# Batch 0 of an attention and feed-forward layer: the second token half of Q and K placed by products with identity columns, W2's Hadamard transform one bank at a time

## Chip, cores and metric

The kernel runs on one core of a Trainium2 chip. The metric is the device time of one execution in microseconds (us). TensorE is called PE in the rows (its weight loads PEld), VectorE DVE, ScalarE ACT, GpSimd POOL; SP is the sync engine, which in this kernel issues every DMA.

## What is computed

The input is x of 4 batches by 512 tokens by 256 features, in float32. Each batch goes through one transformer layer:

```
x = x + layernorm(attention(layernorm(x)))      # 16 heads of 16, rotary positions, causal mask
x = x + layernorm(ffn(layernorm(x)))            # ffn: fwht(silu(x W1') * (x W3')) W2'
```

The attention softmax is over keys up to the query's own position. `fwht` is a Walsh-Hadamard transform of the 1024 hidden features, scaled by 1/32. The kernel folds it into W2 once, at the start, by transforming W2 in place of the hidden values.

## The kernel before

**Numbers in two parts.** Every operand of a product that needs float32 accuracy is held as a high part (the rounded fp32r word) and a low part (value minus high part). A product of two such operands is three products (`triple`, line 280).

**Q and K.** For each of four tiles of 128 tokens, `qkv` (line 399) makes the 512 columns of Q and K, ACT copies them (`copy_qk`), POOL and DVE apply the rotary positions (`rope_products`, line 851; `rope_cos` and `rotate`), PE transposes the result (`turn_qk`, line 426), ACT takes the high part (`qk_high`), DVE the low part (`qk_low`), into `qk_s`: 128 rows (8 heads of 16) by part, by chunk (2 of Q, 2 of K), by token. The scores use another layout. A head there has 48 rows, three for each of the 16 features: high, high, low for Q, and high, low, high for K, so that one product of 48 rows gives the three-term product. Two heads share 96 rows of `q_t`; in `k_t` each head has its own column block and the rows of the other head of the pair are zero. The kernel goes from the one layout to the other through HBM: `pack_qk` (line 298), run by SP, stores `qk_s` to `qk_scratch` in five DMAs per token half (`send`) and reads it back in three (`fetch_k` two, `fetch_q` one). For batch 0 the order is send(0), fetch_k(0), fetch_q(0), then a wait until all three fetches have landed (line 343), send(1), fetch_k(1), fetch_q(1), and after that `load_x(1)`. For batches 1 to 3 this runs beside the feed-forward part of the batch before. For batch 0 there is nothing before it.

**The score units.** The row maxima of the scores are needed before the exponentials. `UNITS` (line 63) is the list of this work: a "scores" unit is one bank of scores of query tile 0 (four heads), tile 1 (two heads), tiles 2 and 3 (one head); a "turn" unit transposes the maxima of a tile, which ACT then writes into rows 96 to 127 of `q_t`. Units 0 to 7 and 9 to 12 are the scores of tiles 0 and 1, which need the first token half alone; units 13 to 29 and 30 to 40 are those of tiles 2 and 3; units 8, 17, 34 and 41 are turns. PE makes a unit, DVE reduces it to maxima (line 1011), and the bank is then free again; batch 0 uses banks 4 to 7 in turn (`FIRST_UNIT_BANKS`). After unit 41, `attend(0)` (line 497) begins: scores transposed, exponentials, values.

**The order of work** is written out by hand: `FIRST_MIX` (line 106) for each engine's part of Q, K and V of batch 0 (q: product and copy, c and r: rotary on DVE, r on PE and ACT: transpose and high part, t: low part, b: values, e: POOL's part of the rotary), and numbers of units after which other work goes in. For batch 0: `FIRST_SELECTOR` (ACT's `select`, 1.9 us each), `BUTTERFLIES_BEFORE` (three stages of the transform of W2 on POOL, two instructions each, line 909), `FIRST_W2_PARTS`: "split" (ACT takes W2's high part, then POOL the low part in two halves, `w2_low`, line 922), "transform" (16 products with the 128 by 128 Hadamard matrix, line 630, into banks 0 to 3), "words" (ACT copies these four banks), "high" (ACT takes the high part of the result; DVE the low part in `iteration(0)`).

**The start.** POOL clears half of `k_t` (line 934), computes the roots of batch 0's first layernorm (`root`), then takes the low part of half of the Q, K and V weights (line 937), for which PE waits (`wqkv_l`). DVE normalizes (`norm_x`, line 1024), takes the low part of the other half of these weights (line 1152), the low parts of the transposed x (line 972) and of the biases (line 1115).

## Time and profile before

| | us |
|---|---|
| median of 3 runs | 493.75 |
| lowest and highest | 491.78, 494.93 |
| the profiled execution | 493.44 |
| its span | 491.7 |
| mean granted clock of TensorE | 0.89 of full speed |

The span is the time from the first to the last recorded instruction; the 1.7 us by which the execution is longer lie around it. Times in the rows count from the start of the span. A row of the timeline gives the start, the length, the engine, the line and the operation; "xN" merges N equal instructions, and the brackets say how long the engine had been idle and what ended that. A waiting instruction's recorded length can include its wait for a resource, which is how a blocked VectorE or GpSimd instruction shows. The clock of 0.50 is 1.2 GHz, 1.00 is 2.4 GHz.

### The profile page before, as it was taken

The page shows a single profiled execution, that of the slowest core. Times are in us where ns is not written, and L with a number is a line of the kernel's source. Part 1 is how long each engine was busy: PE and PEld are TensorE (multiplying, and loading weights), DVE is VectorE, ACT ScalarE, POOL GpSimd, SP SyncE. Part 2 cuts the span into 40 slices and gives each one's busy share as a digit, 9 for nine tenths or more (in the row PEclk, how much of TensorE's full clock was granted, in tenths as well). Part 3 has the DMA queues.
Part 4 walks back from the last instruction along what each step waited for, and adds up shares of the span by engine and source line. Part 5 has one row for each costly group of instructions (what it writes and reads, how often), then busy time and mean ns, then how long its engine had stood idle before and what let it go on. Part 6 is the DMA issues. An engine that isn't in the chain of part 4 may idle for free.

```text
span 491.7 us, 7737 instructions
## 1 busy us (share of the span) xinstructions
PE 406.4 (83%) x2786; PEld 334.9 (68%) x2786; DVE 282.7 (57%) x921; ACT 219.4 (45%) x332; POOL 179.3 (36%) x300
## 2 busy tenths in 40 slices
PE   5656396899599998997799989996899989838992
PEld 4445265459499985576699965585799965527992
DVE  7649377637646678267357677267367782451114
ACT  5436127744423248824423268533333378232221
POOL 5416532733512325614222246325032255132232
PEclk9985557999679999999599999998699999968996
DMA  7676700100785000202981002004950002000001
GB/s 227 221 194 192 171 0 1 45 1 1 204 220 133 1 2 20 67 2 92 231 199 36 2 0 87 1 1 155 239 122 2 1 0 87 0 2 0 1 1 43
DMA packets 35462, 36.94 MB, mean 75 GB/s; under 512 B 2016, under 2 KB 34528, under 8 KB 35424
## 3 DMA queue, kind: packets, MB, share of 16 engines
q1 hardware_dynamic: 35424, 36.45, 26.9%
q8 instruction: 22, 0.36, 0.3%
q14 instruction: 16, 0.13, 0.1%
HBM read 21.76 MB, written 14.68 MB: 74 GB/s over the span
## 4 chain that ended last, share of the span: by engine, by line
PE 58%; DVE 14%; ACT 8%; POOL 8%; issue 6%; DMA 4%; SPq 1%; POOLq 0%; DVEq 0%; ACTq 0%
PE ps L283 32%; PE ps L475 7%; PE ps L463 7%; PE ps L491 6%; DMA q_t<-qk_scratch 3%; ACT probs L704 2%; DVE masked_scores L1011 2%; POOL rstd_z L839 1%; PE ps L525 1%; DVE rot L998 1%; ACT L755 1%; ACT xy L752 1%; POOL w_s L927 1%; PE ps L432 1%; DVE qk_s L972 1%
## 5 line engine op out<-in xcount | busy, mean ns | idle before, releaser
L1011 DVE CUSTOM_DVE_ANT_0 masked_scores<-ps,mask_row 128x128 bf16<-128x128 f32 (+3 forms) x256 | 113.4, 487 | 53.3 <-PE ps L463 53.3
L283 PE MATMUL ps<-xt,w_s 128*128 128x256 f32 x768 | 113.6, 298 | 5.1 <-DVE xt L972 5.1
L283 PEld LDWEIGHTS ps<-xt,w_s 128*128 128x128 f32 x768 | 107.1, 205 | 7.2 <-DVE xt L972 6.9
L463 PE MATMUL ps<-k_t,q_t 96*128 96x128 f32 (+3 forms) x256 | 75.8, 385 | 18.6 <-DMA q_t<-qk_scratch 14.8
L866 POOL TENSOR_TENSOR hid_s<-gate,hid_s 128x512 fp32r<-128x512 f32 x32 | 41.2, 1288 | 120.5 <-ACT hid_s L716 120.5
L704 ACT ACTIVATE probs<-ps 128x1280 f32<-128x1280 f32 x64 | 76.6, 1237 | 11.3 <-PE ps L475 10.4
L463 PEld LDWEIGHTS ps<-k_t,q_t 96*128 96x128 f32 x256 | 47.0, 217 | 29.4 <-DVE maxima L1011 10.2
L475 PEld LDWEIGHTS ps<-q_t,k_t 128*128 128x128 f32 x256 | 44.6, 196 | 30.9 <-ACT probs L704 15.0
L475 PE MATMUL ps<-q_t,k_t 128*128 128x512 f32 (+3 forms) x256 | 54.7, 340 | 4.4 <-ACT probs L704 2.7
L283 PE MATMUL ps<-w_s,hid_s 128*128 128x256 f32 x384 | 54.1, 286 | 3.2 <-POOL hid_s L866 3.2
L283 PEld LDWEIGHTS ps<-w_s,hid_s 128*128 128x128 f32 x384 | 51.1, 193 | 4.3 <-POOL hid_s L866 3.6
L883 POOL TENSOR_SCALAR_AFFINE_SELECT probs<-probs 128x384 f32<-128x384 f32 x64 | 35.9, 561 | 30.8 <-ACT probs L704 30.8
L710 ACT ACTIVATE gate<-ps 128x512 f32<-128x512 f32 x32 | 19.1, 598 | 62.1 <-PE ps L283 62.0
L491 PE MATMUL ps<-probs,v_t 128*32 128x128 f32 (+3 forms) x512 | 43.6, 441 | 1.9 <-POOL probs L886 1.9
L283 PE MATMUL ps<-wqkv_s,q_t 128*128 128x512 f32 (+1 forms) x192 | 43.1, 365 | 1.8 <-ACT v_t L696 0.9
L1085 DVE TENSOR_TENSOR gate<-gate,ps 128x512 f32<-128x512 f32 x32 | 21.9, 685 | 35.7 <-ACT gate L710 35.6
L1018 DVE COPY o_t<-ps 128x512 f32<-128x512 f32 x16 | 11.1, 692 | 46.0 <-PE ps L491 45.6
L283 PEld LDWEIGHTS ps<-wqkv_s,q_t 128*128 128x128 f32 x192 | 32.5, 209 | 6.3 <-ACT v_t L696 1.5
L676 ACT ACTIVATE xt<-ps 128x256 fp32r<-128x256 f32 x32 | 12.1, 382 | 49.5 <-PE ps L534 34.6
L725 ACT ACTIVATE q_t<-ps 32x128 fp32r<-32x128 f32 (+3 forms) x40 | 17.9, 492 | 32.3 <-PE ps L457 32.2
L716 ACT ACTIVATE hid_s<-gate 128x512 fp32r<-128x512 f32 x32 | 20.2, 632 | 25.5 <-DVE gate L1085 22.3
L972 DVE TENSOR_TENSOR xt<-ps,xt 128x256 fp32r<-128x256 f32 x32 | 13.4, 420 | 26.9 <-ACT xt L676 26.6
(111 smaller groups left out, 504.5 us busy)
## 6 DMA issues: line engine op xcount, KB each, us to landing
qk_scratch<-qk_s SPq DMA_DIRECT2D x32, 256.0 KB, 3.5
k_t<-qk_scratch SPq DMA_DIRECT2D x16, 384.0 KB, 5.4
q_t<-qk_scratch SPq DMA_DIRECT2D x8, 768.0 KB, 8.7
qk_scratch<-qk_s SPq DMA_DIRECT2D x8, 512.0 KB, 3.2
xa<-in_x SPq DMA_DIRECT2D x4, 512.0 KB, 9.6
xy<-in_x SPq DMA_DIRECT2D x4, 512.0 KB, 3.6
out<-xy SPq DMA_DIRECT2D x8, 256.0 KB, 2.4
o_t<-in_w SPq DMA_DIRECT2D x1, 1024.0 KB, 10.3
```

Source lines behind the costliest of these rows:

```text
L283: ins = eng.matmul(o, lhs(i), rhs(j), start=first and n == 0, stop=last and n == 2, skip_group_check=skip)
L463: ins = pe.matmul(o[:, i * keys:(i + 1) * keys], q_t[0:QK_ROWS, h // 2, qt * P:qt * P + P], k_t[0:QK_ROWS, h, 0:keys], start=(i == 0), sto ...
L475: ins = pe.matmul(ps[:, col // 512, col % 512:col % 512 + n], k_t[:, h, kt * P:kt * P + P], q_t[:, h // 2, kt * P:TOKENS], start=(kt != 3) ...
L491: ins = pe.matmul(ps[32 * j:32 * j + 32, 6 + g % 2, kt * P:TOKENS], v_t[:, kt, h, :], probs[:, h % PROBS, KEY_COL[kt]:KEY_COL[kt] + TOKENS ...
L704: act.activation(probs[:, h % PROBS, :], src, ACT.Exp, scale=SCALE).then_inc(S["exp_done"], 1)
L710: act.activation(gate[:, a % 2, :], bank(2 * (a % 2)), ACT.Silu).then_inc(S["silu_done"], 1)
L716: act.activation(hid_s[:, a % 2, 0, :], gate[:, a % 2, :], ACT.Copy).then_inc(S["hid_h"], 1)
L866: pool.tensor_tensor(hid_s[:, a % 2, 1, :], gate[:, a % 2, :], hid_s[:, a % 2, 0, :].bitcast(F32), ALU.subtract).then_inc(S["hid_l"], 1)
L883: pool.affine_select(out=v, in_=v, compare_op=ALU.is_ge, fill=0.0, base=0, pattern=[[0, 3], [1, P]], channel_multiplier=-1)
L972: dve.tensor_tensor(dst, src, h.bitcast(F32), ALU.subtract).then_inc(S[done], 1)
L1011: ins = dve.tensor_tensor_reduce(masked_scores[:, SCORE_NO[n] % 2, i * keys:(i + 1) * keys], ps[:, banks[n], i * keys:(i + 1) * keys], mas ...
L1085: dve.tensor_tensor(gate[:, n % 2, :], gate[:, n % 2, :], bank(2 * (n % 2) + 1), ALU.mult)\
```

## The change

For batch 0 alone, the second token half of Q and K no longer goes through HBM.

- POOL clears a region of 2048 columns (the place of W3's low part, unused until later) and fills it by 12 small copies of identity columns: `choose_q` and `choose_k`, matrices that put each of a pair's 16+16 rows at its three places (between `root(0, "x")` and the weights' low part).
- `pick(n)`, 12 of them on PE: four products (two pairs or two heads, high and low part) of 96 columns of that matrix with 256 tokens of `qk_s`, into banks 0 to 3 in turn. `place(n)` copies such a bank into `q_t` or `k_t`: even n on ACT, odd n on DVE. `PICKS_BEFORE` says before which unit each stands, on all three engines.
- SP returns from `pack_qk(0)` after `fetch_q(0)`. So five stores, three fetches and the wait between the halves go, and `load_x(1)` is issued next.
- `FIRST_MIX` is in a new order, the selectors, butterflies and W2's split move, and the transform is done in four pieces of four products, after units 23, 26, 28 and 36, each with a copy of its own.

```diff
 FIRST_MIX = {
-    "PE": """q0 q1 r0 q2 q3 r1 b0 r2 b1 b2 b3 r3""".split(),
-    "ACT": """q0 q1 q2 r0 q3 r1 b0 b1 b2 r2 r3 b3""".split(),
-    "DVE": """c0 r0 c1 r1 t0 c2 c3 r2 t1 r3 t2 t3""".split(),
+    "PE": """q0 q1 r0 q2 q3 r1 b0 b1 r2 b2 b3 r3""".split(),
+    "ACT": """q0 q1 q2 r0 q3 r1 b0 b1 b2 b3 r2 r3""".split(),
+    "DVE": """c0 r0 c1 r1 t0 c2 r2 t1 t2 c3 r3 t3""".split(),
-FIRST_SELECTOR = {2: 0, 3: 2}
-BUTTERFLIES_BEFORE = [0, 4, 13]
-FIRST_W2_PARTS = {"split": 18, "transform": 33, "words": 36, "high": 38}
+FIRST_SELECTOR = {2: 21, 3: 38}
+PICKS = 12
+PICKS_BEFORE = [0, 0, 5, 9, 9, 10, 10, 10, 11, 11, 11, 11]
+BUTTERFLIES_BEFORE = [0, 2, 8]
+FIRST_W2_PARTS = {'split': 10, 'transform': [23, 26, 28, 36], 'words': [31, 33, 38, 38], 'high': 38}
...
                 sp.wait_ge(S["v_done"], b * TILES + TILES)
+                if b == 0:
+                    fetch_q(0)
+                    return
...
                 if kind == "scores" and qt == TILES // 2 and heads[0] == 0:
-                    pe.wait_ge(S["qk_in_late"], (b + 1) * 48)
+                    if b == 0:
+                        pe.wait_ge(S["placed_act"], PICKS // 2)
+                        pe.wait_ge(S["placed_dve"], PICKS // 2)
+                    else:
+                        pe.wait_ge(S["qk_in_late"], b * 48)
...
+            def pick(n):
+                if n == 0:
+                    pe.wait_ge(S["picks_made"], 1)
+                    pe.wait_ge(S["qk_l"], TILES)
+                    pe.wait_ge(S["v_copied"], TILES)
+                if n >= 4:
+                    pe.wait_ge(S["placed_act" if n % 2 == 0 else "placed_dve"], (n - 4) // 2 + 1)
+                for i in range(2):
...
+                    for part in range(2):
+                        ins = pe.matmul(ps[0:QK_ROWS, n % 4, i * DIM:i * DIM + DIM], columns[part],
+                                        qk_s[:, part, chunk, TOKENS // 2:TOKENS], start=(i == 0 and part == 0),
+                                        stop=(i == 1 and part == 1), skip_group_check=True)
+                ins.then_inc(S["picked"], 1)
...
             pool.memset(k_t[0:QK_ROWS, 0:HEADS // 2, :].bitcast(F32), 0.0).then_inc(S["zeroed"], 1)
+            pool.memset(chooser.bitcast(F32), 0.0).then_inc(S["chooser_zero"], 1)
             root(0, "x")
+            pool.wait_ge(S["eye_in"], 16)
+            pool.wait_ge(S["chooser_zero"], 1)
+            rows = ident[:, :].rearrange("p (a e w) -> p a e w", a=4, e=2)
+            for part, terms_q, terms_k in ((0, (0, 1), (0, 2)), (1, (2,), (1,))):
+                for j in terms_q:
+                    to = choose_q[part].rearrange("p a (e w j) -> p a e w j", e=2, j=3)[:, :, :, :, j]
+                    for e in range(2):
+                        pool.tensor_copy(to[:, :, e, :], rows[:, :, e, :])
+                for j in terms_k:
...
+                        ins = pool.tensor_copy(to[:, :, 2 * e, :], rows[:, :, e, :])
+            ins.then_inc(S["picks_made"], 1)
             pool.wait_ge(S["split_h"], 1)
             pool.tensor_tensor(wqkv_s[:, 1, 1, :], raw_wqkv[:, 3 * DIM:6 * DIM], wqkv_s[:, 0, 1, :].bitcast(F32), ALU.subtract)\
```

## Rows read from the trace of the kernel before

**Rows 1.** Windows of batch 0's start: stretch, length, busy us by engine, clock, DMA.

```profile
41.20:50.00 8.80, 8.36 (x33) 7.30 (x33) 8.80 (x56) 4.14 (x5) 5.02 (x4) 0.50 0.57 186
50.00:58.30 8.30, 0.07 (x1) 0.00 (x0) 1.55 (x10) 0.22 (x1) 6.02 (x4) 0.50 1.06 231
68.00:72.00 4.00, 3.95 (x18) 3.94 (x19) 1.25 (x6) 0.06 (x1) 0.08 (x1) 0.50 0.00 0
73.00:74.00 1.00, 0.94 (x4) 0.52 (x3) 1.00 (x5) 0.98 (x2) 0.00 (x0) 0.96 0.00 0
```

**Rows 2.** The chain that ended last, in order of time: start, us, what.

```profile
33.90 7.25 DMA q_t<-qk_scratch
...
49.38 8.92 DMA q_t<-qk_scratch
...
68.05 3.75 PE ps L635 x16
...
76.76 0.20 ACT max_s L736
```

**Rows 3.** Timeline of GpSimd, VectorE and TensorE, 0.8 to 16 us.

```profile
0.96 3.51 POOL L934 MEMSET k_t<- 96x4096 f32 x1
9.64 1.85 POOL L937 TENSOR_TENSOR wqkv_s<-raw_wqkv,wqkv_s 128x768 fp32r<-128x768 f32 x1 [0.27 <-ACT wqkv_s L773]
12.21 0.95 DVE L1152 TENSOR_TENSOR wqkv_s<-raw_wqkv,wqkv_s 128x768 fp32r<-128x768 f32 x1
13.64 1.60 PE L283 MATMUL ps<-wqkv_s,q_t 128*128 128x512 f32 x6 [0.85 <-DVE q_t L972]
15.62 0.47 PE L411 MATMUL ps<-bias_s,sixty_fourth 128*128 128x512 f32 x1 [0.38 <-DVE bias_s L1115]
```

**Rows 4.** Source line 1024, 8 to 30 us: shortest, median and longest, in ns.

```profile
L1024 DVE TENSOR_SCALAR xa<-xa,rstd_x,shift_x x4: 402/408/1912, 9.4 to 11.9; 128x256 f32<-128x256 f32 x4
```

**Rows 5.** Timeline of GpSimd and VectorE, 90 to 104 us, then 37 to 43 us.

```profile
96.36 2.69 POOL L883 TENSOR_SCALAR_AFFINE_SELECT probs<-probs 128x384 f32<-128x384 f32 x1 [0.39 <-ACT probs L704]
99.00 0.29 POOL L886 TENSOR_SCALAR_AFFINE_SELECT probs<-probs 128x128 f32<-128x128 f32 x1
...
96.39 2.28 DVE L1120 TENSOR_TENSOR w_s<-raw_w,w_s 128x2048 fp32r<-128x2048 f32 x1
...
37.63 2.45 POOL L919 TENSOR_TENSOR mixed_w<-o_t 128x1024 f32<-128x1024 f32 x1 [10.90 <-DVE wo_s L1120]
...
40.40 2.26 DVE L1164 CAST had_s<-had 128x128 fp32r<-128x128 f32 x1
42.58 0.28 DVE L1011 CUSTOM_DVE_ANT_0 masked_scores<-ps,mask_row 128x128 bf16<-128x128 f32 x1
```

**Rows 6.** Timeline of SP's DMA issues, 31 to 51 us.

```profile
31.70 0.85 SPq L325 DMA_DIRECT2D k_t<-qk_scratch  x2
...
48.50 0.84 SPq L325 DMA_DIRECT2D k_t<-qk_scratch  x2
...
49.90 0.54 SPq L292 DMA_DIRECT2D xa<-in_x  x1
```

**Rows 7.** Timeline of ScalarE and VectorE, 33 to 37 us: the last tile's parts.

```profile
34.74 0.60 ACT L676 ACTIVATE qk_s<-ps 128x512 fp32r<-128x512 f32 x1 [1.54 <-PE ps L432]
35.38 0.69 DVE L972 TENSOR_TENSOR qk_s<-ps,qk_s 128x512 fp32r<-128x512 f32 x1 [1.44 <-ACT qk_s L676]
```

**Rows 8.** VectorE's score reductions, timeline 51 to 73 us.

```profile
51.47 0.08 DVE L1011 DVE_READ_ACCUMULATOR2_ANT maxima<- 128x1 f32 x1
...
59.07 0.56 DVE L1011 CUSTOM_DVE_ANT_0 masked_scores<-ps,mask_row 128x384 bf16<-128x384 f32 x1 [7.53 <-PE ps L463]
...
72.48 0.69 DVE L1011 CUSTOM_DVE_ANT_0 masked_scores<-ps,mask_row 128x512 bf16<-128x512 f32 x1 [3.23 <-PE ps L463]
```

**Rows 9.** Rows that price a pick (PE) and its copy (DVE), timeline and source view.

```profile
24.72 0.96 PE L283 MATMUL ps<-wqkv_s,q_t 128*128 128x256 f32 x6
...
L1018 DVE COPY o_t<-ps x16: 691/692/692, 94.2 to 423.6; 128x512 f32<-128x512 f32 x16
```

More of the change, by code:

```diff
@@ L245, in layer_kernel @@
         raw_w3 = xy[:, :, :, :].rearrange("p a b c -> p (a b c)")
+        chooser = w3_s[:, 1, :, :].rearrange("p c n -> p (c n)")
+        choose_q = [chooser[:, n * 384:n * 384 + 384].rearrange("p (a m) -> p a m", a=4) for n in range(2)]
+        choose_k = [chooser[:, 768 + n * 576:768 + n * 576 + 576].rearrange("p (a m) -> p a m", a=4) for n in range(2)]
         maxima = sb("maxima", [P, 2, HEADS])
@@ L628, in feed_forward, with transform @@
                         score_unit(b + 1, n, UNIT_BANKS)
-            def transform():
+            def pick(n):
[6 more added lines that the diff above has]
+                for i in range(2):
+                    if n < PAIRS // 2:
+                        pair, chunk = 2 * n + i, (2 * n + i) // 4
+                        columns = [t[:, pair % 4, :] for t in choose_q]
+                    else:
+                        head = 2 * (n - PAIRS // 2) + i
+                        chunk = CH + head // 8
+                        columns = [t[:, head // 2 % 4, HEAD_ROWS * i:HEAD_ROWS * i + QK_ROWS] for t in choose_k]
+                    for part in range(2):
[3 more added lines that the diff above has]
+                ins.then_inc(S["picked"], 1)
+            def transform(piece):
                 pe.wait_ge(S["had_made"], 1)
                 pe.wait_ge(S["w2_l"], 2)
-                for c in range(HCH):
+                for c in (2 * piece, 2 * piece + 1):
                     for part in range(2):
@@ L649, in _ @@
             for n in range(N_UNITS):
+                for p in range(PICKS):
+                    if PICKS_BEFORE[p] == n:
+                        pick(p)
                 score_unit(0, n, FIRST_UNIT_BANKS)
-                if n == FIRST_W2_PARTS["transform"]:
-                    pe.wait_ge(S["v_copied"], TILES)
-                    transform()
+                for piece in range(4):
+                    if n == FIRST_W2_PARTS["transform"][piece]:
+                        pe.wait_ge(S["v_copied"], TILES)
+                        transform(piece)
             pe.wait_ge(S["made_sel"], 4)
             pe.wait_ge(S["ones_made"], 1)
-            pe.wait_ge(S["transformed_words"], 1)
+            pe.wait_ge(S["transformed_words"], 4)
             for b in range(BATCHES - 1):
@@ L773, in split, with place @@
                 act.activation(w[:, 0, :, :].rearrange("p c n -> p (c n)"), raw, ACT.Copy).then_inc(S["split_h"], 1)
+            def place(n):
+                act.wait_ge(S["picked"], n + 1)
+                to = (q_t[0:QK_ROWS, 2 * n:2 * n + 2, TOKENS // 2:TOKENS] if n < PAIRS // 2 else
+                      k_t[0:QK_ROWS, 2 * n - PAIRS:2 * n - PAIRS + 2, TOKENS // 2:TOKENS])
+                act.activation(to, ps[0:QK_ROWS, n % 4, :].rearrange("p (a t) -> p a t", a=2), ACT.Copy)\
+                   .then_inc(S["placed_act"], 1)
             def select(n):
@@ L798, in _ @@
             for n in range(N_UNITS):
+                for p in range(0, PICKS, 2):
+                    if PICKS_BEFORE[p] == n:
+                        place(p)
                 score_unit(0, n, FIRST_UNIT_BANKS)
@@ L805, in _ @@
                     act.activation(w2_s[:, 0, :, :].rearrange("p c n -> p (c n)"), mixed_w2, ACT.Copy).then_inc(S["w2_h"], 1)
-                if n == FIRST_W2_PARTS["words"]:
-                    act.wait_ge(S["transformed"], 1)
-                    act.activation(raw_w2, ps[:, 0:4, :].rearrange("p a n -> p (a n)"), ACT.Copy, scale=W2_SCALE)\
-                       .then_inc(S["transformed_words"], 1)
+                for piece in range(4):
+                    if n == FIRST_W2_PARTS["words"][piece]:
+                        act.wait_ge(S["transformed"], piece + 1)
+                        act.activation(raw_w2[:, piece * 512:piece * 512 + 512], bank(piece), ACT.Copy, scale=W2_SCALE)\
+                           .then_inc(S["transformed_words"], 1)
                 if n == FIRST_W2_PARTS["high"]:
-                    act.wait_ge(S["transformed_words"], 1)
+                    act.wait_ge(S["transformed_words"], 4)
                     act.activation(w2_s[:, 0, :, :].rearrange("p c n -> p (c n)"), raw_w2, ACT.Copy)\
@@ L1145, in iteration, with place @@
                 feed_forward(b, steps)
+            def place(n):
+                dve.wait_ge(S["picked"], n + 1)
+                to = (q_t[0:QK_ROWS, 2 * n:2 * n + 2, TOKENS // 2:TOKENS] if n < PAIRS // 2 else
+                      k_t[0:QK_ROWS, 2 * n - PAIRS:2 * n - PAIRS + 2, TOKENS // 2:TOKENS])
+                dve.tensor_copy(to, ps[0:QK_ROWS, n % 4, :].rearrange("p (a t) -> p a t", a=2)).then_inc(S["placed_dve"], 1)
             dve.memset(k_t[0:QK_ROWS, HEADS // 2:HEADS, :].bitcast(F32), 0.0).then_inc(S["zeroed"], 1)
@@ L1166, in _ @@
             for n in range(N_UNITS):
+                for p in range(1, PICKS, 2):
+                    if PICKS_BEFORE[p] == n:
+                        place(p)
                 score_unit(0, n, FIRST_UNIT_BANKS)
```

9 lines of the change are left out of this document (5 added, 4 removed).

## The prediction

> **What bounds the kernel now.** Read the chain of waits first [rows 2], then the windows around the places it names [rows 1], then the timeline of each engine there. In batch 0 the chain runs twice through a fetch of `q_t` from HBM: issued at 33.90 for the first token half (7.25 us) and at 49.38 for the second (8.92 us, landed at 58.30). The window 50.00 to 58.30 shows what the second costs: PE busy 0.07 us of 8.30, DVE 1.55, with the DMA engines full [rows 1]. The change takes this round trip away. Around it VectorE is the limit: in 41.20 to 50.00 it is busy 8.80 of 8.80 us. Its own rows give the stage a skeleton [rows 8]: units 0 to 12 from 42.58 [rows 5] to 51.55 (8.9 us), idle 7.53 us, units 13 to 33 from 59.07, idle 3.23 us, then six units of tile 3 at 0.61 each from 72.48, to 76.2. The second idle time lies behind the 16 transform products at 68.05, 3.75 us of PE [rows 2]. So at most 7.5 + 3.2 = 10.7 us stand idle on VectorE before `attend(0)` starts, 1.4 us after ACT has read the last maxima at 76.76 [rows 2]. The question is how much of it comes back after the new work, and what that work delays. After `attend(0)` both kernels do the same in the same order, so I carry the shift of its start to the end: the sum is made against the profiled execution, 493.44 us, which is 0.3 below the median 493.75 and 1.7 above its span.
>
> **1. The chooser at the start.** The clearing of 2048 columns costs 3.51 / 2 = 1.8 us by the clearing of 4096 [rows 3]; it begins at 4.5 and ends at 6.3, before GpSimd's root work at 8.1, so it costs nothing (if it took twice as long, still nothing). The 12 copies of 64 elements are another matter. They stand ahead of GpSimd's low part of the weights, for which PE waits with the first product of Q and K. Before, this began at 9.64 after an idle 0.27, so GpSimd was free at 9.37; it took 1.85 and ended at 11.49, and PE began at 13.64 for other reasons (DVE's weights and xt) [rows 3]. That is 2.15 us of slack. The trace has no GpSimd copy; the nearest one-input operation, 128 columns, took 0.29 [rows 5]. I take 0.24 each, 12 x 0.24 = 2.9 us. Bounds: 0.17 (2.0 us) and 0.35 (4.2 us), the latter if the steps of 3 words slow it. Beside them VectorE does four normalizations (0.40 us) and its weights' low part (0.95). Do the two engines stand in each other's way? The trace says yes: one normalization took 1.91 us instead of 0.40 while GpSimd took the weights' low part [rows 4, 3], a one-input GpSimd operation took 2.69 us beside a two-input VectorE one of 2.28 [rows 5], and the copy of the Hadamard matrix, 2.26 us, sat behind a butterfly [rows 5]. So up to 4 x 0.40 + 0.95 = 2.5 us of VectorE's time is added to GpSimd's; I take 1.6, since part of an operation's length is not the shared part. GpSimd's weights part then starts at 9.4 + 2.9 + 1.6 = 13.9 and ends at 15.75. PE's first tile: 15.8 + 1.60 + 0.4 (bias product) = 17.8 instead of 16.1, so **+1.7 us**. The rest of the stage is one chain of copy, rotary, transpose, parts, so this shift goes all the way down. Bounds: 0 (cheap copies and no contention: 9.4 + 2.0 + 1.85 = 13.3, inside the slack) and +4 (4.2 + 2.5, and the biases' low part, 0.95, gets in front: 9.4 + 7.6 + 1.85 = 18.9, plus 2.0, less 16.1 = 4.8, of which I doubt the last 0.8).
>
> A page says the same as a rule: the Trainium skill, "SBUF — State Buffer", "Who interferes with whom", has VectorE and GpSimd sharing one port pair as a lock held for a whole instruction, taken by VectorE's two-input operations and its fast copy modes, and an operation with at most one SBUF input outside these modes stays free. By it the five operations above collide with all 12 copies, and the copies of PSUM banks in step 3 collide with nothing; without it, from the rows alone, the second point is that the 16 copies of a 512-column bank all took 0.69 [rows 9].
>
> **2. The new order of the mix.** ACT's high part of tile 2 now stands behind all four copies of V, and VectorE does c3, r3 after t2. So tile 3's chain (c3 0.69, r3 0.69, transposes 0.63, high part 0.60, low part 0.69) starts at about 33.3 and ends near 36.6, where the low part ended at 36.07 [rows 7]: **+0.5**, between -0.6 and +1.0. On it hang the output weights' low part, then butterfly 0 (37.63) and the Hadamard copy behind it, at whose end VectorE begins unit 0, at 42.58 [rows 5], although the first scores' operands had landed at 41.15. V is complete some 2 us earlier, but this buys nothing: the first half's k fetch was issued at 31.70 [rows 6] and waits for stores, of which at most 0.3 us goes; and `load_x(1)` now follows q at once, as it did in the second half, where k at 48.50, q, x at 49.90 [rows 6] needed 9.8 us from k's issue to q's landing, against 9.45 in the first. So the landing is at 31.7 - 0.3 + 1.7 + 9.8 = 42.9, still hidden: VectorE's first unit would start at 42.58 + 1.7 + 0.5 = 44.8. It first places pick 1, 0.62: **45.4**.
>
> **3. Units 0 to 12 with the picks.** A pick is four products of 256 columns. At 1.2 GHz 16 such products took 3.75 us [rows 2], 0.94 a pick; at 2.4 GHz six took 0.96 [rows 9], 0.64 a pick. A place is 0.6 on ACT [rows 7] and, for 512 columns, 0.69 on VectorE [rows 9], less some 0.07 as its last part overlaps. VectorE: 8.9 for the units plus 5 x 0.62 = 3.1 for places 3 to 11 (odd). PE is the rival for the bound: nine picks (3 to 11) stand between units 8 and 12. The turn (unit 8) waits for GpSimd's low part of the maxima, which now stands behind butterfly 1 (two instructions of 2.35), so PE leaves it near 49.9. Then five picks at 0.94, with the clock low, until dense work lifts it as the transform did (0.50 in 68.00 to 72.00, busy 3.95 of 4 us, then 0.96 in 73.00 to 74.00 [rows 1]), four at 0.64 and four units at 0.4: 4.7 + 2.6 + 1.6 = 8.9, to 58.8; place 11 and units 11 and 12 follow. In this arrangement VectorE is idle 2.9 us in several pieces between 51 and 58. Unit 13 starts at 45.4 + 8.9 + 3.1 + 2.9 = **60.3**, against 59.07: +1.2. All of the 7.5 us of idle time is spent: 1.7 + 0.5 + 0.6 + 3.1 + 2.9 = 8.8. If PE stays at 1.2 GHz, four picks cost 0.3 more each (+1.2); if it is at 2.4 from the start, the 2.9 us shrink to about 0.8 and later pieces cost nothing (step 4).
>
> **4. Units 13 to 41.** VectorE's work is 10.1 (59.07 to 69.25 [rows 8]) + 3.7 = 13.8 us. The pieces of the transform, 0.94 each at 1.2 GHz, are covered by the three units PE is ahead, 1.4 us, but PE regains only 0.13 us per unit (0.48 on VectorE against 0.35 on PE), so the second to fourth piece show by some 0.5 each, with a little from tile 3: 1.9 us instead of 3.2. Unit 40 ends at 60.3 + 13.8 + 1.9 = 76.0, against 76.2. Then ACT is late: after unit 34's rows (near 70.8 to 71.9) it has the last selector 1.9, two word copies 0.6 each and the high part 1.9, to 76.9. The maxima of unit 40 were read at 76.76, also behind a high part [rows 2]. So `attend(0)` starts 76.9 - 76.76, rounded up, **+0.2** late. The earlier split, butterflies and selectors hide in ACT's and GpSimd's idle time; the price if the split's wait for butterfly 2 (near 55) delayed places 8 and 10 past pick 11 is 0.6, counted in the range. Sum: 493.44 + 0.2 = 493.6 us.
>
> **The rivals.** (a) *PE is at 2.4 GHz from the first picks on.* For: nine picks, 36 products of 256 columns, with little between them. Against: 8.36 us busy of 8.80 in 41.20 to 50.00 left it at 0.50 [rows 1]. Time: 2.9 - 0.8 = 2.1 saved in step 3 and 1.9 in step 4, of which ACT's end (unit 29's end plus 7.4 us) leaves 2.9 in all: 490.7. (b) *The chooser is free*, GpSimd's copies being short and the lock short with them: 1.7 less, 491.9; with (a), 489.0. (c) *Slower: the chooser is dear.* Twelve copies at 0.35 and all of VectorE's 2.5 us before the weights' part give step 1 +4 instead of +1.7: 495.9. It decides as soon as GpSimd's weights part ends after 15.9, since from there each us is one us of the end. For: every product of Q and K waits for it, and nothing later has slack. Against: short operations of this engine took 0.2 to 0.3. (d) *PE stays at 1.2 GHz through all picks*: +1.2 and 0.3 in step 4, 495.1. (e) *The change doesn't do what it says*, the idle time before unit 13 remaining because the places are late: that is (d) with ACT blocked by the split; no more than 0.6 on top.
>
> **How the numbers follow.** The forecast, between 492.6 and 494.8, has 0.42; (a) 0.17, (b) 0.13, both together 0.05, (c) 0.13, (d) and (e) 0.10. A step of a few us cannot be told from none here below about 1%, 4.9 us, which is what a measurement of this kernel resolves. Faster by over 1% (below 488.8) needs (a) and (b) and another us, and I allow for a start that hides more than I see: 0.10. Slower by over 1% (above 498.7) needs (c) and (d) in full: 0.05. Within 1%: 0.85. The range from 490.0 to 497.0 takes in (a), (b) and (c) and leaves out their sums.
>
> **What would show it.** In the profile after: GpSimd's weights part ending near 15.8 and PE's first product of Q and K with it (step 1; at 13.6 it is (b)); VectorE's first unit near 45.4, the DMA engines idle after some 44 us; unit 13 near 60.3, with the clock at 0.50 until some 54 us; `attend(0)` near 78.4; no wait on `q_t`'s second fetch. The prediction is wrong if `attend(0)` starts before 76 or after 81, or if the stages after it change length by over 1 us, which I take to be nil.

## The result, and the profile after

The changed kernel takes 487.52 us (median of 4 runs, 487.19 to 488.27) where the kernel before took 493.70 beside it (4 runs, 491.78 to 494.93): a ratio of 0.988, with a 95% interval from 0.986 to 0.990. Forecast were 493.6 us and a range from 490.0 to 497.0; the gain is 6 us, and the time lies below the range. The profiled execution, the slowest of the four, took 488.27 us with a span of 486.4, 5.2 and 5.3 us less than before. `attend(0)` starts at 73.80 instead of 78.20; that is 4.4 us of it, and the other 0.9 lie behind it, where I had allowed for none.

The start first: the timeline of the changed kernel for GpSimd, VectorE, TensorE and ScalarE, 9 to 17 us, beside [rows 3].

```profile
9.30 1.04 POOL L993 CAST w_s<-ident 128x64 fp32r<-128x64 f32 x4
9.40 1.46 DVE L1087 TENSOR_SCALAR xa<-xa,rstd_x,shift_x 128x256 f32<-128x256 f32 x4 [1.41 <-POOL shift_x L891]
10.26 1.96 POOL L997 CAST w_s<-ident 128x64 fp32r<-128x64 f32 x4
10.78 0.95 DVE L1223 TENSOR_TENSOR wqkv_s<-raw_wqkv,wqkv_s 128x768 fp32r<-128x768 f32 x1
...
12.86 1.80 POOL L1000 TENSOR_TENSOR wqkv_s<-raw_wqkv,wqkv_s 128x768 fp32r<-128x768 f32 x1
...
14.72 1.65 PE L289 MATMUL ps<-wqkv_s,q_t 128*128 128x512 f32 x6 [3.03 <-POOL wqkv_s L1000]
...
16.64 0.60 ACT L729 ACTIVATE qk_b<-ps 128x512 f32<-128x512 f32 x1 [2.92 <-PE ps L418]
```

The copies (CAST, 64 columns) do stand ahead of GpSimd's part of the weights, and TensorE does wait for it now. But it begins at 12.86, not 13.9, and the first copy of Q and K is 0.52 us late (16.12 before), not 1.7. The normalizations, one of which had been held up to 1.91 us by GpSimd's weights part [rows 4], now run in 1.46 us for all four, with the short copies beside them instead.

The chain of waits of the changed kernel, 33 to 74 us (start, us, what), beside [rows 2]:

```profile
33.11 9.06 DMA q_t<-qk_scratch
42.17 0.04 issue
42.21 4.21 PE ps L474 x18
46.42 0.85 PE ps L658 x4
47.28 1.28 PE ps L474 x6
48.56 0.11 PE ps L468
48.66 1.76 PE ps L658 x8
50.42 0.43 PE ps L474 x2
50.85 1.43 PE ps L658 x12
...
66.41 1.06 ACT q_t L762 x2
67.50 1.91 ACT k_t L823
69.43 1.09 ACT o_t L857 x2
70.57 1.79 issue
72.36 0.20 ACT max_s L773
```

One fetch of `q_t` is left in it, the second is gone, and L658 (the picks) stands in the place of the second. The end of the stage is ScalarE's: rows, selector, the words of the last two pieces and the high part (the "issue" of 1.79 lies within it), and only then the last maxima. Behind the pieces of the transform VectorE waits little. Its longest waits between unit 0 and unit 40, from the timeline of VectorE (in brackets):

```profile
47.74 0.42 DVE L1074 CUSTOM_DVE_ANT_0 masked_scores<-ps,mask_row 128x256 bf16<-128x256 f32 x1 [0.18 <-PE ps L474]
...
50.89 0.43 DVE L1074 CUSTOM_DVE_ANT_0 masked_scores<-ps,mask_row 128x256 bf16<-128x256 f32 x1 [0.39 <-PE ps L474]
...
63.13 0.56 DVE L1074 CUSTOM_DVE_ANT_0 masked_scores<-ps,mask_row 128x384 bf16<-128x384 f32 x1 [0.29 <-PE ps L474]
...
64.60 0.56 DVE L1074 CUSTOM_DVE_ANT_0 masked_scores<-ps,mask_row 128x384 bf16<-128x384 f32 x1 [0.42 <-PE ps L474]
...
71.19 0.08 DVE L1074 DVE_READ_ACCUMULATOR2_ANT maxima<- 128x1 f32 x1
```

That is 1.3 us, and 1.5 with the shorter gaps, where 7.53 + 3.23 stood [rows 8]. The account of VectorE: units 0 to 40 took from 42.58 to 76.2 before, 33.6 us, and now from 43.43 to 71.27, 27.8. That is 5.8 us less: 9.2 of idle time are gone (10.75 less 1.5), and 3.45 are spent on five places, 0.69 each. Take off the later start (0.85) and what ScalarE is later than VectorE at the end (1.1 us now, 0.5 before, by the reading at 76.76), and 4.4 us are left.

In the windows of the changed kernel the clock column (0.50, 0.94, 0.66) shows where the picks ran at which level; VectorE is busy 6.42 of 6.60 and 5.81 of 6.40 us in the two stretches of units 0 to 12.

```profile
43.40:50.00 6.60, 6.60 (x32) 6.55 (x32) 6.42 (x50) 1.88 (x4) 6.60 (x4) 0.50 0.01 2
50.00:56.40 6.40, 5.77 (x41) 5.16 (x40) 5.81 (x20) 4.07 (x5) 4.37 (x3) 0.94 0.00 0
56.40:66.40 10.00, 9.10 (x31) 7.30 (x31) 9.24 (x39) 4.37 (x7) 3.17 (x4) 0.66 0.00 0
```

And TensorE's picks in its timeline: at 48.46 eight products take 1.96 us, at 52.35 sixteen take 2.04, that is 0.98 and 0.51 us a pick of four.

```profile
48.46 1.96 PE L658 MATMUL ps<-qk_s,w_s 128*96 128x256 f32 x8
...
50.65 1.63 PE L658 MATMUL ps<-qk_s,w_s 128*96 128x256 f32 x12
...
52.35 2.04 PE L658 MATMUL ps<-qk_s,w_s 128*96 128x256 f32 x16
```

### The profile page after: what moved, and what is told of

It reads as the page before. It is cut to its first block, busy times and chain, and to the rows that moved or that the text cites. A ratio compares the mean times of both kernels' runs of the same rounds, so it can differ in the third digit from the quotient of the medians.

```text
span 486.4 us, 7859 instructions
## 1 busy us (share of the span) xinstructions
PE 407.2 (84%) x2834; PEld 338.4 (70%) x2834; DVE 286.1 (59%) x927; ACT 222.7 (46%) x341; POOL 184.2 (38%) x313
## 4 chain that ended last, share of the span: by engine, by line
PE 60%; DVE 13%; ACT 8%; POOL 8%; issue 6%; DMA 3%; SPq 1%; POOLq 0%; DVEq 0%; ACTq 0%
PE ps L289 32%; PE ps L474 9%; PE ps L486 7%; PE ps L502 6%; ACT probs L741 2%; DMA q_t<-qk_scratch 2%; DVE masked_scores L1074 2%; PE ps L658 1%; POOL rstd_z L888 1%; PE ps L536 1%; DVE rot L1061 1%; ACT L792 1%; ACT xy L789 1%; ACT qk_s L713 1%; PE ps L439 1%
## 5 line engine op out<-in xcount | busy, mean ns | idle before, releaser
L474 PE MATMUL ps<-k_t,q_t 96*128 96x128 f32 (+3 forms) x256 | 73.3, 366 | 7.1 <-DMA q_t<-qk_scratch 2.3
L474 PEld LDWEIGHTS ps<-k_t,q_t 96*128 96x128 f32 x256 | 45.3, 211 | 16.1 <-DVE maxima L1074 9.7
L289 PE MATMUL ps<-wqkv_s,q_t 128*128 128x512 f32 (+1 forms) x192 | 42.0, 358 | 4.0 <-POOL wqkv_s L1000 3.0
L439 PE MATMUL ps<-ident,rot 128*128 128x128 f32 x64 | 13.2, 343 | 19.8 <-DVE rot L1061 15.5
```

Of the source, the lines that this page charges most:

```text
L289: ins = eng.matmul(o, lhs(i), rhs(j), start=first and n == 0, stop=last and n == 2, skip_group_check=skip)
L439: ins = pe.transpose(ps[:, 7, c * P:c * P + P], rot[:, t % 2, c * P:c * P + P], ident[:, :])
L474: ins = pe.matmul(o[:, i * keys:(i + 1) * keys], q_t[0:QK_ROWS, h // 2, qt * P:qt * P + P], k_t[0:QK_ROWS, h, 0:keys], start=(i == 0), sto ...
```

## The experiments

In four groups, each on one chip with the kernel before beside it. The table gives the points of batch 0 from one profile of each (us from the start of the span): VectorE's first unit, its unit 13, ScalarE's reading of the last maxima, the start of `attend(0)`; then the median and the ratio to the kernel before.

| kernel | unit 0 | unit 13 | maxima | `attend(0)` | median | ratio, 95% |
|---|---|---|---|---|---|---|
| before | 42.58 | 59.07 | 76.76 | 78.20 | 493.7 | |
| changed | 43.43 | 56.41 | 72.36 | 73.80 | 487.5 | 0.986–0.990 |
| e1_old_w2_plan | 43.44 | 56.41 | 77.39 | 78.83 | 496.1 | 1.001–1.006 |
| e2_pieces_alone | 44.28 | 61.01 | 76.48 | 77.93 | 492.7 | 0.993–0.998 |
| e3_old_mix | 44.05 | 56.53 | 72.54 | 73.99 | 489.4 | 0.987–0.991 |
| e4_transform_at_once | 44.94 | 57.40 | 75.91 | 79.36 | 496.4 | 1.003–1.009 |
| e5_weights_first | 44.69 | 57.91 | 73.89 | 75.33 | 490.1 | 0.987–0.994 |
| e6_chooser_twice | 48.73 | 61.86 | 77.83 | 79.28 | 492.6 | 0.995–0.999 |
| e7_selector_early | 45.44 | 58.62 | 73.55 | 75.01 | 490.0 | 0.988–0.994 |
| e8_three_moves | 45.71 | 59.12 | 74.05 | 75.67 | 491.4 | 0.988–0.995 |
| e9_x_after_landing | 43.67 | 56.46 | 72.27 | 73.71 | 488.1 | 0.986–0.992 |
| e10_busy_start | 44.59 | 57.29 | 72.22 | 73.67 | 489.2 | 0.988–0.993 |
| e11_busy_before_scores | 43.47 | 56.21 | 72.19 | 73.64 | 488.2 | 0.987–0.993 |
| e12_three_moves_x | 42.95 | 55.84 | 70.70 | 72.16 | 488.9 | 0.987–0.993 |
| e13_changed_again | 43.06 | 55.91 | 71.84 | 73.29 | 489.1 | 0.988–0.993 |
| e14_moves_x_busy_start | 44.38 | 56.58 | 71.22 | 72.69 | 490.0 | 0.988–0.992 |

The kernel before had 493.8 us beside e1 to e4, 494.9 beside e5 to e8, 494.3 beside e9 to e12 and 494.4 beside e13 and e14.

### Which part of the change pays

**e1: the picks with the old plan for W2.**

```diff
-FIRST_SELECTOR = {2: 21, 3: 38}
-BUTTERFLIES_BEFORE = [0, 2, 8]
-FIRST_W2_PARTS = {'split': 10, 'transform': [23, 26, 28, 36], 'words': [31, 33, 38, 38], 'high': 38}
+FIRST_SELECTOR = {2: 0, 3: 2}
+BUTTERFLIES_BEFORE = [0, 4, 13]
+FIRST_W2_PARTS = {'split': 18, 'transform': [33, 33, 33, 33], 'words': [36, 36, 36, 36], 'high': 38}
```

> The changed kernel, but with the plan of before for W2 (split after unit 18, butterflies before units 0, 4 and 13, all 16 transform products after unit 33, copies after 36, selectors after units 0 and 2). Theory: the picks bring unit 13 forward to about 56.4 us, but the third butterfly then waits for GpSimd's part of unit 12's maxima and ends near 61.7, W2's high part near 63.6, its low part near 68.4, so the transform still starts at 68.4 and attend(0) near 78.6, as before: 493.9 us, no gain from the picks alone. Rival, the gain is the saved round trip: unit 13 is 2.7 us earlier than before and everything behind keeps that: 491.0 us.

Unit 13 comes at 56.41 as in the changed kernel, and yet `attend(0)` starts at 78.83, later than before. The timeline of e1 for GpSimd, ScalarE and TensorE, 59 to 75 us:

```profile
59.32 2.36 POOL L969 TENSOR_TENSOR mixed_w<-o_t 128x1024 f32<-128x1024 f32 x1
61.72 1.91 ACT L853 ACTIVATE w_s<-mixed_w 128x2048 fp32r<-128x2048 f32 x1 [3.21 <-POOL mixed_w L969]
63.71 4.64 POOL L976 TENSOR_TENSOR w_s<-mixed_w,w_s 128x1024 fp32r<-128x1024 f32 x2 [2.02 <-ACT w_s L853]
...
68.50 3.75 PE L668 MATMUL ps<-w_s,had_s 128*128 128x256 f32 x16 [3.51 <-POOL w_s L976]
```

The 2.7 us that the picks give at unit 13 are lost again to a second chain: butterfly, split (the high part of W2), low part, transform. Before, this chain ran in the shadow of the fetch, and the transform began at 68.05 [rows 2]; it still begins at 68.50. Without the fetch it is the bound.

**e2: the pieces and the early plan alone**, on the kernel before (the round trip through HBM stays). The transform and its copies are divided in four as in the change; of that the lines below show only the plan.

```diff
-FIRST_SELECTOR = {2: 0, 3: 2}
-BUTTERFLIES_BEFORE = [0, 4, 13]
-FIRST_W2_PARTS = {"split": 18, "transform": 33, "words": 36, "high": 38}
+FIRST_SELECTOR = {2: 21, 3: 38}
+BUTTERFLIES_BEFORE = [0, 2, 8]
+FIRST_W2_PARTS = {'split': 10, 'transform': [23, 26, 28, 36], 'words': [31, 33, 38, 38], 'high': 38}
...
```

> The kernel before with the new plan for W2 (early split and butterflies, four pieces, later selectors), still with the second half through HBM and the old mix order. Theory: unit 13 starts at 59.1 as before; VectorE's idle 3.2 us at the transform shrinks to 1 to 1.5; the last maxima are read near 74.6 instead of 76.8, so 2.2 us less: 491.5 us. Rival (the pieces are hidden anyway, the gain is all in the picks): 493.7.

From unit 13 to the maxima 15.5 us instead of 17.7: the pieces are worth 2.2 us there. In the time 0.4% is left. Its profiled execution lost 1.6 us at the start of the kernel, which has nothing to do with the edit: the copy of tile 2 came at 23.97 instead of 22.38. The window 20.00 to 24.00 of e2 shows where:

```profile
20.00:24.00 4.00, 3.92 (x12) 3.26 (x13) 1.85 (x3) 0.03 (x1) 0.61 (x1) 0.57 0.02 7
```

The granted clock is 0.57 there and TensorE gets 12 products done; before it was 1.00 and 18 products. TensorE had been idle 2.4 us ahead of it in both.

The three together say what the change is: e1 alone costs 0.3%, e2 alone gains 0.4%, both gain 1.2%. The picks alone do not pay, and the two together gain more than the sum of each alone, since each takes away one of two waits that cover each other.

**e3: the old order of the mix** (`FIRST_MIX` as before, all else changed).

> The changed kernel with the mix order of before. Theory: tile 3's low part ends near 36.6 either way, V being earlier buys nothing since q's landing is hidden behind VectorE: 487.7 us, within 0.5 of the changed kernel's 487.5. Rival (the new order is worth a microsecond, through V or through TensorE's clock, which stayed at 2.4 GHz over V's products): 488.7 or more.

Unit 0 comes at 44.05 instead of 43.43, `attend(0)` at 73.99 instead of 73.80: in these two profiles the new order is worth 0.2 us. The times say more: 488.3 to 489.8 us, every one above the changed kernel's 487.2 to 488.3, and the median 1.9 us higher, as the rival had it. But the profiled execution is the fastest of e3's four, and the changed kernel's own times spread more than that in e13. So whether the new order is worth 0.2 us or over 1 stays open. It let q's fetch be issued at 33.11 instead of 34.72, but the fetch landed at the same time, 42.1; that its packets stand behind k's would explain it and was not shown.

**e4: the transform in one go**, all else as changed.

```diff
-FIRST_W2_PARTS = {'split': 10, 'transform': [23, 26, 28, 36], 'words': [31, 33, 38, 38], 'high': 38}
+FIRST_W2_PARTS = {'split': 10, 'transform': [33, 33, 33, 33], 'words': [36, 36, 36, 36], 'high': 38}
```

> The changed kernel with its early split and butterflies, but all 16 transform products after unit 33 and the four copies after 36. Theory: VectorE's idle time at the transform is back at 3.2 us (2 if TensorE is at 2.4 GHz there) instead of 1.0: 489.5 us, between 488.5 and 490. Rival (moving the split early did it all, and pieces are worth nothing): 487.5.

A miss: `attend(0)` starts at 79.36. A low clock at the start, as in e2 (0.57 between 20 and 24 us), makes 1.0 us of it at unit 13. The rest, in the timeline of e4, 70 to 79 us, of ScalarE, VectorE, GpSimd and TensorE:

```profile
70.08 2.06 ACT L857 ACTIVATE o_t<-ps 128x512 f32<-128x512 f32 x4
72.17 1.91 ACT L823 ACTIVATE k_t<-sel 32x2048 fp32r<-32x2048 f32 x1
74.09 1.91 ACT L861 ACTIVATE w_s<-o_t 128x2048 fp32r<-128x2048 f32 x1
75.91 0.19 ACT L773 ACTIVATE max_s<-maxima 128x10 fp32r<-128x10 f32 x1
76.04 2.29 DVE L1183 TENSOR_TENSOR w_s<-o_t,w_s 128x2048 fp32r<-128x2048 f32 x1 [1.21 <-ACT w_s L861]
76.18 2.21 POOL L923 TENSOR_TENSOR max_s<-maxima,max_s 128x10 fp32r<-128x10 f32 x1 [10.50 <-ACT max_s L773]
...
79.36 1.09 PE L486 MATMUL ps<-q_t,k_t 128*128 128x512 f32 x2 [0.55 <-ACT q_t L762]
```

I had counted the pieces as a stall of VectorE (3.2 us at once or 0.5 each). They also spread ScalarE's words: in one go all of the words, the selector and the high part, 5.9 us, stand behind the transform and ahead of the last maxima. And the high part then ends as VectorE is free, so VectorE's low part of W2 starts ahead of GpSimd's subtraction of the maxima, which takes 2.21 us instead of 0.22. The Trainium skill, "SBUF — State Buffer", "Who interferes with whom", has a rule for this: a VectorE operation with both inputs in SBUF contends with a GpSimd operation that reads SBUF, for one pair of ports, which is an exclusive lock. These two rows agree with it (2.29 us of VectorE, 2.21 us of GpSimd); no run here parts it from other causes.

### What the chooser costs

**e5: GpSimd's part of the weights ahead of the chooser.** The lines from `pool.wait_ge(S["eye_in"], 16)` to `ins.then_inc(S["picks_made"], 1)`, copies and all, move behind GpSimd's `tensor_tensor` that makes its part of `wqkv_s`.

> The changed kernel with GpSimd's low part of the weights ahead of the 12 chooser copies instead of behind them. Theory: the copies then stand in GpSimd's idle time before the rotary products; ScalarE's first copy of Q and K begins at 16.1 us as in the kernel before instead of 16.6, and everything up to attend(0) moves by the same 0.5: attend(0) at 73.3, 487.0 us. Rival (the chooser costs 1.7 us of the start, as predicted): 485.9; rival (hidden): 487.5.

The first copy of Q and K (ScalarE) is at 16.27 and the last low part at 35.52 instead of 16.64 and 35.86. At the first copy the chooser's price of some 0.4 us is borne out by more profiles: 16.19 to 16.27 in the four with the weights first (e5, e8, e12, e14), 16.62 to 16.75 in eight with the chooser first, among them the changed kernel's; only e6 and e7 are later. At the last low part it is not: e13, the changed kernel again, has it at 35.50 too. There the clock was low between 16 and 20 us, the copy of tile 1 was late (19.71), GpSimd's next rotary products stood behind VectorE's first rotary sum instead of beside it, and this sum took 0.69 us instead of 1.19. In time nothing came through, as the first fetch landed at 43.50 and VectorE waited 1.52 us for it; so the 490.1 us say nothing on the chooser.

**e6: the 12 copies twice**, the second set into unused columns of W2's low part, with `picks_made` counted to 2.

> The changed kernel with the 12 chooser copies made twice (the first time into W2's low part, where nothing reads them). Theory: 12 more copies at 0.24 to 0.30 us, VectorE's normalizations being over: GpSimd's weights part ends 2.9 to 3.6 later, at about 17.9, the first copy of Q and K begins at 19.8 instead of 16.6, and attend(0) at 77.0 instead of 73.8, microsecond for microsecond: 490.8 us. Rival (the start has slack further down, in the landing of the first half or VectorE's blocked copies): under 489.5.

The timeline of e6 for GpSimd, 12 to 18 us:

```profile
12.71 0.80 POOL L1007 CAST w_s<-ident 128x64 fp32r<-128x64 f32 x4
13.42 0.80 POOL L1011 CAST w_s<-ident 128x64 fp32r<-128x64 f32 x4
14.14 1.17 POOL L1007 CAST w_s<-ident 128x64 fp32r<-128x64 f32 x2
15.23 0.45 POOL L1011 CAST w_s<-ident 128x64 fp32r<-128x64 f32 x2
15.60 1.80 POOL L1014 TENSOR_TENSOR wqkv_s<-raw_wqkv,wqkv_s 128x768 fp32r<-128x768 f32 x1
```

The second set puts GpSimd's weights part off by 2.74 us (15.60 against 12.86), TensorE's first product by 2.73, and the last low part by 3.3; the 0.5 between them is TensorE's, whose clock was 0.50 from 17 to 22 us here and 1.00 in the changed kernel. `attend(0)` starts 5.5 us later, 2.0 of it behind a late landing as in e5, and the ratio goes from 0.988 to 0.997. So there is no slack left: rival (c) had its mechanism right, and only the chooser's size keeps it away. The set also prices copies that nothing holds up: (13.42 - 12.71) / 4 = 0.18 us each, beside VectorE's low parts of the transposed x, which read one of their two inputs from PSUM.

### What is late next

**e7: selector part 3 behind unit 24 instead of 38.** `FIRST_SELECTOR = {2: 21, 3: 24}`

> The changed kernel with ScalarE's last selector after unit 24 instead of after unit 38. Theory: at the end of the units ScalarE is the last engine (selector 1.9, two word copies 1.1, high part 1.9 behind unit 34's rows), 1.1 us behind VectorE's last maxima; without the selector there the last maxima are read at 71.3 instead of 72.4: attend(0) at 72.7, 486.4 us. Rival (VectorE's units are the bound all through): 487.5.

The last maxima are read as soon as VectorE has them, and from unit 0 to there it takes 28.1 us instead of 28.9. The 0.8 us were used up at the front by a late landing (44.24).

**e8: e5, e7, and the copy of the Hadamard matrix ahead of the output weights' low part.**

> The changed kernel with three moves: weights before chooser, last selector after unit 24, and VectorE's Hadamard copy and output biases ahead of the output weights' low part, so that the first butterfly can't block them. Theory: VectorE's first unit comes when the first half has landed and PE has made a unit, about 42.5 instead of 43.4 (0.5 of it from the start), the last maxima are read at 70.4: attend(0) at 71.8, 485.5 us. Rival (the butterflies start later and W2's parts with them, so that the transform's pieces or the high part wait): 486.5 or more.

The copy now takes 0.23 us at 38.45 instead of 2.26 at 40.65, and VectorE is idle 5.12 us until the landing at 44.51. Wherever VectorE waits for the landing, unit 0 begins 1.2 us behind it (e5, e8, e9, e12). In the changed kernel that would be 43.37, and behind the Hadamard copy and the place it was 43.43: the copy was never the limit by itself, two waits ended together there.

**e9: `load_x(1)` behind the landing.**

```diff
             pack_qk(0, EARLY_SEND[0])
+            sp.wait_ge(S["qk_in"], 48)
             load_x(1)
```

> The changed kernel, with SyncE waiting for the landing of batch 0's first half of q and k before it issues load_x(1). My theory (load_x(1), issued 0.5 us behind q's fetch, stretches it from 7.3-7.5 us to 9.1-10.8 us, and since the chooser is cheap this landing now decides VectorE's first unit about as late as the Hadamard copy does): q's fetch lands 7.2 to 7.8 us after its issue, and where the landing was last (42.17 in the changed kernel, VectorE's first place at 42.83) the first unit begins 0.3 to 1.5 us earlier than in the changed kernel, bound by the Hadamard copy alone, at 43.0 or before; time 486 to 487.5 in a run whose start is as in the changed kernel's. Rival (the length of the fetch is its own packets', 128-word pieces, and x behind it costs nothing): landing 9 us or more after the issue, unit 0 and the time unchanged.

The chain of e9:

```profile
33.08 9.39 DMA q_t<-qk_scratch
```

9.39 us with nothing behind it: my theory falls as I put it. The 7.3 us were the wrong measure, since q was then issued 2.2 us behind k. Counted from the issue of k's first half to q's landing there are 9.5 us before, 9.7 in e2, 10.3 in e9, 9.9 in e12 and 9.8 in e14 without `load_x(1)` behind, and with it 10.0 in the changed kernel and e1, 9.8 in e3, 9.7 in e4, 9.6 in e10 and e11, 9.9 in e13, but 11.6 in e5 and e6, 11.7 in e7 and 11.3 in e8. These four ran on one chip, and no profile of another chip has more than 10.3. So it may be the chip, or the load on that chip; the wait was not tried there, and this stays open.

**e10: TensorE busy at the start.** Ahead of the first `turn_qk`, in its idle time, with a result that nobody reads:

```diff
+                        if b < 0 and t == 0:
+                            for _ in range(8):
+                                pe.matmul(bank(6), wqkv_s[:, 0, 0, 0:P], wqkv_s[:, 0, 0, 0:2 * DIM], start=True, stop=True,
+                                          skip_group_check=True)
```

> The changed kernel, and behind the second product of Q and K (TensorE idle 2.4 us there until the rotary result comes, at 18.05 to 20.57) eight products of 512 columns whose result nobody reads. My theory (in a part of the executions the granted clock falls to its lower level behind this idle time, and products at 1.2 GHz then cost 1.5 us up to the copy of tile 2, as in three profiles so far, 24.4 against 22.9): no execution with a low clock between 20 and 24 us, copy of tile 2 at 22.9 to 23.1, and the times lie closer together, none of the upper group; the median at or below the changed kernel's, 486.5 to 487.6. Rival (the lower clock at 20 us comes from elsewhere, say from the chip's state, and not from this idle time): the upper group is as frequent as in the kernel before on the same chip, and the profile can show 0.5 there all the same.

The clock was 1.00 between 20 and 24 us, but so it was in the changed kernel's profile. The six times lie between 488.2 and 489.6, no lower than the changed kernel's. Unexpected, and not explained by any run: the last store of the first half landed 4.8 us after its issue instead of 3.2, so k's fetch was issued at 33.81 instead of 32.21, and unit 0 began 1.2 us later. e14 shows the same (4.9). `attend(0)` was not late for it: ScalarE's chain at the end took up what VectorE lost.

**e11: TensorE busy before the scores**, five products of the same form between pick 1 and unit 0.

> The changed kernel, and between picks 1 and unit 0 five products of 512 columns whose result nobody reads, at 1.2 GHz 2.1 us, which fill TensorE's idle time 39.9 to 42.2. It asks what the clock is still worth in the stage of the picks. My theory (the clock rises some time after TensorE has become busy without a break; in the changed kernel it was busy from 42.2 and rose at 50.5): with these the clock rises by some 2 to 4 us earlier, near 47 to 48, all picks run warm (0.52 instead of 0.98 us each), but VectorE was idle only 0.7 us in the stage, so unit 13 begins at most 0.7 us earlier and the time falls by 0.3 to 1 us. Rival (the clock would bring the whole stage forward, as the part of the forecast on 1.2 GHz had it): 2 us or more. If the products delay unit 0, up to 0.5 us are lost.

The clock in the windows of e11:

```profile
49.00:50.00 1.00, 1.00 (x6) 1.00 (x6) 1.00 (x5) 0.39 (x1) 1.00 (x1) 0.50 0.00 0
50.00:51.00 1.00, 1.00 (x8) 1.00 (x7) 0.77 (x4) 0.59 (x1) 1.00 (x2) 0.63 0.00 0
51.00:52.00 1.00, 1.00 (x11) 1.00 (x10) 0.88 (x3) 0.37 (x1) 1.00 (x1) 1.00 0.00 0
```

TensorE was busy without a break from 37.88, and the clock rose at 50.6 all the same, as in the changed kernel, where it had been idle from 39.9 to 42.2. Unit 13 came at 56.21, 0.2 us earlier. Both theories expected an earlier rise from filling that time, and both were wrong on it. What makes it rise there is open.

**e12: e8 with e9's wait.**

> The kernel of e8 (weights' low part before the chooser, selector part 3 behind unit 24, Hadamard copy before the output weights' low part) with load_x(1) behind the landing as in e9. In e8 VectorE was idle 5.1 us before unit 0 and waited for q's landing alone, 10.4 us after its issue. My theory: landing 7.2 to 7.8 us after the issue, near 40.5 to 41.5 by the start's clock, unit 0 at 42 to 42.7 (e8: 45.7), maxima read by 71, attend(0) near 71.5 to 72.5 against 75.7 in e8; time 484 to 486.5, the fastest so far. Rival: the fetch still takes 10 us, time as e8's, 491.

The earliest `attend(0)` of all, 72.16, with VectorE bound by the landing at 41.77, and then by its own work to the end (the chain ends on its maxima at 70.70, not on ScalarE). The profiled execution took 487.18 us, but the median is 488.9, and from `attend(0)` to the end it gave 0.5 us back (span 485.3 less 72.16 is 413.1, against 412.6 in the changed kernel).

**e13: the changed kernel again, and e14: e12 with e10's products.**

> The changed kernel without any edit, beside e14 on the same chip. It serves to compare: 487.2 to 488.3 us so far (4 runs, on another chip), attend(0) at 73.8. Theory: 487.5 to 488.5 again, q's landing 9.5 to 10 us after k's issue as in the first trace. Rival (load_x(1) right behind can stretch the fetches by some 1.5 us, as in e5, e7 and e8, and whether it does differs from execution to execution): 11 us or more here, with the first unit at 44.5 or later.

> The kernel of e12 with the eight products of e10 behind the second product of Q and K. By e12's trace attend(0) starts 1.6 us before the changed kernel's, but its median time was no better than that of e9. Theory (the times of e12 lie in two groups, 486.7 to 487.2 and 488.7 to 489.6, and the upper one is made by the granted clock falling near 20 us, which these products prevent): all times within 1 us of each other, near 486.5, 1 us or more below e13's. Rival (the spread comes from later stages, where the phases of the clock fall differently): the same spread as e12's, median 488 to 489 and no better than e13's.

The changed kernel's six times were 487.7, 487.8, 487.8, 490.4, 490.7 and 490.8; those of e14 487.4, 487.5, 489.9, 490.0, 490.4 and 490.4. Keeping TensorE busy near 20 us does not take away the upper group, so the theory that the clock there makes it falls. The profiles say the same. The window 16.00 to 20.00 of e13 has a clock of 0.57, where the changed kernel's first profile had 1.00:

```profile
16.00:20.00 4.00, 3.67 (x10) 2.37 (x8) 1.24 (x2) 0.89 (x2) 1.93 (x2) 0.57 0.80 325
```

Yet this execution belongs to the lower group, with 487.81 us; and e4's profile, with 0.57 between 20 and 24 us, is the second fastest of its ten. What makes the upper group is open.

The landing came 9.9 us after k's issue in e13, as the theory had it. The lower groups of the changed kernel here, e12 and e14 lie between 486.7 and 487.8: no version measurably beats the changed kernel. Its gain stands at 5 to 6 us: the ratio is 0.988 on one chip and 0.990 on another.

## Why the prediction was wrong

What bounds the kernel before was read rightly: the round trip and the transform on VectorE's idle time, 10.7 us as the most there was to gain. It failed in what was taken off that sum. The forecast put `attend(0)` at 78.4 and it started at 73.8, 4.6 us earlier. Two terms make nearly all of it, each with 2.0: the late start of VectorE's units (steps 1 and 2, mis-sized) and the wait for the picks (step 3, where the mechanism failed). Step 4 makes the other 0.6.

- **Step 1, "so this shift goes all the way down", +1.7 us: right in kind, too large.** Measured +0.5. From 9.30 to 12.86 the 12 copies took 3.56 us and not 4.5. By the copies of e6, 0.18 us each, that is 2.15 us of copies instead of 2.9, and 1.4 of contention where I took 1.6: the copies' price was off, hardly the contention. Its parts are told by the starts of the groups of four, 0.96 and 1.87 us apart against 0.71: the first group, beside normalizations of 0.40, lost 0.25; the second lost 1.16, nearly all in one copy that took 1.28 (from 10.58) beside the weights' low part (10.78 to 11.73).
- **Step 2, +0.5 us: the size was wrong.** The last low part ended at 36.55, 0.5 behind before, all of it from step 1, and at VectorE's place ahead of unit 0 only 0.25 of it were left (42.83 where unit 0 stood before, at 42.58). Steps 1 and 2 had 2.2 there. This makes the first unit 43.43 instead of 45.4: 2.0 us. The landing at 42.17 was hidden, as forecast, but barely: VectorE's Hadamard copy ended at 42.9, and e5, e7 and e8 are what happens when it is not.
- **Step 3, "VectorE is idle 2.9 us in several pieces": this is the step that failed.** Measured 0.8, by the two windows above (6.60 less 6.42 and 6.40 less 5.81). Units 0 to 12 took 13.0 us instead of 14.9. The work was nearly as forecast, 8.9 + 3.1 against 12.2; the wait for the picks was not. I let five picks run at 0.94 and put the clock's rise at 54; two ran at 0.98, and the clock had risen by 51. A fast pick, priced at 0.64 by the six products of 256 columns [rows 9], took 0.52. Two picks at the low level and seven at the high one make 5.6 us where 4.7 + 2.6 stood, and from the turn to the end of unit 12 TensorE needed 6.4 us (48.46 to 54.87) instead of 8.9. Why the clock rose when it did, e11 did not find. Rival (a), full clock from the first pick, is wrong too: three of the picks after unit 0 were at the low level. The truth lay between, and VectorE's idle time was that of (a), 0.8 us.
- **Step 4, 1.9 us of stalls: too large.** Measured 0.7: two of the four pieces showed, by 0.29 and 0.42; the last, 0.64 us long at the higher clock, did not. That ScalarE would be last, with the selector, the words and the high part, was right: it was 1.1 us late. In all 15.95 us instead of 16.6.
- **"The stages after it ... I take to be nil": 0.9 us less.** 413.5 us from `attend(0)` to the end before, 412.6 after, with no edit in them. The same code takes from 412.4 (e3) to 414.3 us (e1, e4) in the other profiles, so the 0.9 lies within what it differs by, and is luck as far as the change goes. Two steps of it can be seen, 0.22 us near 83 and 0.27 near 141 us of the kernel before: there the clock rose later than at the same work of the changed kernel (0.79 in 82.90 to 83.90 against 1.00 in 78.50 to 79.50; 0.67 in 140.70 to 141.70 against 0.98 in 136.04 to 137.04).
- **Step 4, "the earlier split, butterflies and selectors hide in ACT's and GpSimd's idle time".** They do, but what I did not see is that the gain rests on them: in e1, without them and the pieces, it is nil. I had the two waits one behind the other in the chain and did not ask what the second hung on when the first moves: on GpSimd's third butterfly, planned for unit 13.
- **The chances.** Rivals (a) and (b) together, 489.0 us, had 0.05, and the range left them out. They do not exclude each other, and nearly both happened: the picks cost VectorE what (a) said, the chooser a third of the forecast. The profiled execution took 488.27. I had priced four uncertain losses (1.7, 0.5, 2.9, 1.9), which together gave back 7 of 10.7 us, and let the range hold an error in one of them at a time. A time faster by over 1% (below 488.8), which is what came, had 0.10.

## What to carry over

When a change removes a long wait, list what ran in its shadow and when each of these ends without it: here the transform's chain through GpSimd would have taken the whole gain (e1), and only the second edit, worth 0.4% by itself (e2), let the first one pay. When several estimated losses are taken off a gain, the range has to hold the sum of their errors, and rivals that can come true together are no alternatives.
